# Matrix fill of a graph kernel: which engine makes the one-hots, which sums, which stores

## The reference

```python
def _L2_gnn_ref(emb, edge_weight, row, col, num_layers):
    w = edge_weight[:, None]
    X = emb
    for _ in range(num_layers):          # 3
        msgs = w * X[col]                # col = dst
        X = jax.ops.segment_sum(msgs, row, num_segments=n)   # row = src
    return X
x = _layernorm(x + _L2_gnn_ref(x, edge_weight, src, dst, 3), axis=-1)
```

## Time and profile before

| | |
|---|---|
| median of three runs | 10728.15 us (10725.5 to 10730.36) |
| the profiled execution | 10736.09 us |
| its span, first to last instruction | 10734.2 us |
| mean granted clock of TensorE | 0.844 |
| busy share of the span: PE, DVE, ACT, POOL | 72%, 67%, 15%, 49% |
| fill stage | 3294 to 4591 us of the span |

### The profile page before, as it was taken

How to read it: one execution, slowest core, us unless ns; L and a number is a source line. 1 busy time by engine, 2 the same in 40 slices (tenths; PEclk the granted TensorE clock), 3 DMA queues, 4 the chain that set the end, 5 groups by cost and what they waited for, 6 DMA issues and landing times. The chain is left out here.

```text
span 10734.2 us, 171530 instructions
## 1 busy us (share of the span) xinstructions
PE 7773.0 (72%) x33251; PEld 5843.1 (54%) x33252; DVE 7167.4 (67%) x12981; ACT 1583.2 (15%) x4852; POOL 5236.8 (49%) x6235
## 2 busy tenths in 40 slices
PE   0888869899987777756666649866664986666488
PEld 0788859788874444423444426644442664444256
DVE  2233346799955666601888779778876987888688
ACT  0222211233320000001111111211110121111011
POOL 1677720477735777700777700077771006777100
PEclk9999999899975555566999869799986988999698
DMA  5333341122231222274555641055565105555510
GB/s 23 52 61 60 61 51 40 37 46 46 46 26 65 91 91 91 91 294 177 137 137 137 129 84 37 31 133 137 137 133 89 37 26 129 137 137 136 92 40 23
DMA packets 1413038, 947.03 MB, mean 88 GB/s; under 512 B 916255, under 2 KB 1276696, under 8 KB 1412435
## 3 DMA queue, kind: packets, MB, share of 16 engines
q0 software_dynamic: 184960, 458.42, 19.9%
q1 hardware_dynamic: 1131794, 427.96, 17.0%
q10 hardware_dynamic: 96192, 59.54, 1.7%
HBM read 697.23 MB, written 248.11 MB: 88 GB/s over the span
## 5 line engine op out<-in xcount | busy, mean ns | idle before, releaser
L845 PE MATMUL ps<-rows,ohT 128*128 x7040 | 2173.4, 449 | 1348.3 <-DMA gx<-table_g,gi 670.8
L629 POOL DMA_INDIRECT gx<-table_g,gi x2640 | 2500.6, 947 | 806.0 <-issue 726.9
L845 PEld LDWEIGHTS ps<-rows,ohT 128*128 128x128 f32 x7040 | 1444.5, 248 | 1917.0 <-DMA gx<-table_g,gi 980.9
L1134 PE MATMUL ps<-work,oh 128*128 128x273 f32 (+1 forms) x7040 | 1780.1, 409 | 346.0 <-DVE oh L648 340.1
L1134 PEld LDWEIGHTS ps<-work,oh 128*128 128x128 f32 x7040 | 1342.8, 228 | 782.3 <-issue 436.1
L614 POOL COPY gi<-src_i 128x16 int32 (+1 forms) x280 | 57.4, 205 | 2476.1 <-POOLq L508 2413.8
L1630 PE MATMUL ps<-oh 128*128 128x196 f32 x2352 | 1007.9, 584 | 290.7 <-DVE oh L1597 287.1
L734 DVE TENSOR_TENSOR work<-gx,ps 128x768 f32<-128x768 f32 x660 | 629.9, 954 | 732.3 <-PE ps L847 731.8
L1099 DVE TENSOR_TENSOR work<-rows,xl 128x1024 f32<-128x1024 f32 (+1 forms) x880 | 871.6, 990 | 321.5 <-DMA xl<-xs_g 145.7
L795 ACT CAST ohT<-ps 128x512 f32<-128x512 bf16 x888 | 520.4, 586 | 3639.8 <-PE ps L828 3636.9
L1619 POOL TENSOR_SCALAR oh<-gx,lin 128x196 f32<-128x196 f32 x1176 | 902.7, 780 | 286.0 <-PE ps L1630 284.6
(11 more groups left out here) (305 smaller groups left out, 8744.7 us busy)
## 6 DMA issues: line engine op xcount, KB each, us to landing
big<-dense_d SPq DMA_DIRECT2D x96, 784.0 KB
dense_d<-big SPq DMA_DIRECT2D x588, 98.0 KB
dense_d<-big ACTq DMA_DIRECT2D x588, 98.0 KB
gx<-table_g,gi POOLq DMA_INDIRECT x2640
xs_g<-gx SPq DMA_DIRECT2D x660, 64.0 KB
xl<-xs_g SPq DMA_DIRECT2D x660, 64.0 KB, 1.8
rows<-dense_d SPq DMA_DIRECT2D x48, 784.0 KB
type_d<-work SPq DMA_DIRECT2D x220, 96.0 KB
```

What stands on the lines that cost most here:

```text
L629: pool.indirect_dma_start(m.gx[:, u, k, 0:w], None, table, bass.IndirectOffsetOnAxis(m.gi[:, odd, u * K + k:u * K + k + 1].bitcast(U32), 0 ...
L845: ins = nc.tensor.matmul(to, turned, rows, start=True, stop=not adds)
L1134: ins = nc.tensor.matmul(sums(u), m.oh[:, u, k, :], rhs(u % 2)[:, k, :], start=(k == 0), stop=(k == K - 1))
```

## The change

The fill is spread anew over the engines.

- ScalarE makes the row one-hots, without weights, in two ACTIVATEs each: `far = Square(iota + bias)` with the bias the negated key, then `spots = Relu(1 - far)`, which is 1 where the two are equal and 0 elsewhere. Every turn it first copies four keys to `lin`. So that the bias is ready, `dense_plan` writes `v_key` negated (same instruction, other signs).
- GpSimd's column one-hot takes the weight as a second operation, `is_equal` then `mult`, and copies four weights per turn beside the four numbers.
- VectorE only sums. The order one-hot, sum is gone from its queue.
- SyncE issues all four stores of a turn. It reads the four home numbers of a turn with one call at the head of the turn, and its loop is not written out for the first two turns. ScalarE issues no store.

TensorE's product waits for `spot` in place of `hot`, otherwise it stays as it was.

```diff
@@ -1518,8 +1518,8 @@
             nc.vector.tensor_copy(m.v_home[:, :], home)
             dve.wait_ge(s("picked"), 1)
             for k in range(3):
-                nc.vector.scalar_tensor_tensor(out=m.v_key[:, third(k)], in0=win_no[:, third(k)], scalar=-float(P),
-                                               in1=bank(3 + k), op0=ALU.mult, op1=ALU.add).then_inc(s("v_keys"), 1)
+                nc.vector.scalar_tensor_tensor(out=m.v_key[:, third(k)], in0=win_no[:, third(k)], scalar=float(P),
+                                               in1=bank(3 + k), op0=ALU.mult, op1=ALU.subtract).then_inc(s("v_keys"), 1)
 
         @block.scalar
         def _(act):
@@ -1570,7 +1570,10 @@
     spots = m.one_hots[:, 0:RING * P].rearrange("p (n q) -> p n q", n=RING)
     at = RING * P
     his = m.one_hots[:, at:at + RING * HIS].rearrange("p (n h) -> p n h", n=RING)
+    at += RING * HIS
+    far = m.one_hots[:, at:at + RING * P].rearrange("p (n q) -> p n q", n=RING)
     sums = m.big[:, 0:RING * HIS].rearrange("p (n h) -> p n h", n=RING)
+    numbers, weights, keys = m.lin[:, 0, 0:RING], m.lin[:, 0, RING:2 * RING], m.lin[:, 1, 0:RING]
     turns = VISITS // RING
 
     def before(u):
@@ -1582,7 +1585,7 @@
 
         @block.vector
         def _(dve):
-            def add(i, u):
+            def body(i, u):
                 v = i * RING + u
                 dve.wait_ge(s("made"), v + 1)
                 need(dve, s("summed"), v)
@@ -1590,67 +1593,67 @@
                 nc.vector.scalar_tensor_tensor(out=sums[:, u, :], in0=sums[:, before(u), :],
                                                scalar=m.v_keep[:, bass.ds(v, 1)], in1=m.ps[:, u, 0:HIS],
                                                op0=ALU.mult, op1=ALU.add).then_inc(s("summed"), 1)
-
+            nc.vector.memset(sums[:, RING - 1, :], 0.0).then_inc(s("blank"), 1)
+            dve.wait_ge(s("blank"), 1)
+            groups(dve, body, turns)
+
+        @block.scalar
+        def _(act):
             def body(i, u):
                 v = i * RING + u
-                need(dve, s("made"), v - RING + 1)
-                nc.vector.tensor_scalar(spots[:, u, :], m.iota_row[:, :], m.v_key[:, bass.ds(v, 1)],
-                                        m.v_w[:, bass.ds(v, 1)], ALU.is_equal, ALU.mult).then_inc(s("hot"), 1)
-                if u:
-                    add(i, u - 1)
-                elif not isinstance(i, int) or i:
-                    add(i - 1, RING - 1)
-            nc.vector.memset(sums[:, RING - 1, :], 0.0)
-            groups(dve, body, turns)
-            add(turns - 1, RING - 1)
+                if not u:
+                    need(act, s("far"), v)
+                    nc.scalar.copy(keys, m.v_key[:, bass.ds(v, RING)]).then_inc(s("keys"), 1)
+                    act.wait_ge(s("keys"), i + 1)
+                need(act, s("spot"), v - RING + 1)
+                nc.scalar.activation(far[:, u, :], m.iota_row[:, :], ACT.Square, bias=keys[:, u:u + 1]
+                                     ).then_inc(s("far"), 1)
+                act.wait_ge(s("far"), v + 1)
+                need(act, s("made"), v - RING + 1)
+                nc.scalar.activation(spots[:, u, :], far[:, u, :], ACT.Relu, bias=m.ones[:, 0:1], scale=-1.0
+                                     ).then_inc(s("spot"), 1)
+            groups(act, body, turns)
 
         @block.gpsimd
         def _(pool):
-            numbers = m.lin[:, 0, 0:RING]
-
             def body(i, u):
                 v = i * RING + u
                 if not u:
                     need(pool, s("high"), v)
                     nc.gpsimd.tensor_copy(numbers, m.v_hi[:, bass.ds(v, RING)]).then_inc(s("numbers"), 1)
-                    pool.wait_ge(s("numbers"), i + 1)
+                    nc.gpsimd.tensor_copy(weights, m.v_w[:, bass.ds(v, RING)]).then_inc(s("numbers"), 1)
+                    pool.wait_ge(s("numbers"), 2 * (i + 1))
                 need(pool, s("made"), v - RING + 1)
                 pool.sem_inc(s("place"), 1)
-                nc.gpsimd.tensor_scalar(his[:, u, :], m.hi_no[:, :], numbers[:, u:u + 1], None, ALU.is_equal
-                                        ).then_inc(s("high"), 1)
+                nc.gpsimd.tensor_scalar(his[:, u, :], m.hi_no[:, :], numbers[:, u:u + 1], weights[:, u:u + 1],
+                                        ALU.is_equal, ALU.mult).then_inc(s("high"), 1)
             groups(pool, body, turns)
 
         @block.tensor
         def _(pe):
             def body(i, u):
                 v = i * RING + u
-                pe.wait_ge(s("hot"), v + 1)
+                pe.wait_ge(s("spot"), v + 1)
                 pe.wait_ge(s("high"), v + 1)
                 need(pe, s("summed"), v - RING + 1)
                 nc.tensor.matmul(m.ps[:, u, 0:HIS], spots[:, u, :], his[:, u, :], start=True, stop=True
                                  ).then_inc(s("made"), 1)
             groups(pe, body, turns)
 
-        def store(eng, slots):
-            def body(i, u):
-                if u not in slots:
-                    return
-                v = i * RING + u
-                home = eng.value_load(m.v_home[0:1, bass.ds(v, 1)], min_val=0, max_val=NWIN + RING - 1)
-                eng.wait_ge(s("summed"), v + 1)
-                eng.dma_start(m.dense_d.rearrange("(w p) h -> w p h", p=P)[bass.ds(home, 1)].rearrange("a p h -> (a p) h"),
-                              sums[:, u, :]).then_inc(s(f"stored{u}"), 16)
-            groups(eng, body, turns)
-            for u in slots:
-                eng.wait_ge(s(f"stored{u}"), 16 * turns)
-
         @block.sync
         def _(sp):
-            store(sp, (0, 2))
-
-        @block.scalar
-        def _(act):
-            store(act, (1, 3))
+            view = m.dense_d.rearrange("(w p) h -> w p h", p=P)
+
+            with sp.Fori(0, turns, 1) as i:
+                _, homes = nc.values_load_multi_w_load_instructions(
+                    m.v_home[0:1, bass.ds(i * RING, RING)], engines=(mybir.EngineType.SP,), min_val=0,
+                    max_val=NWIN + RING - 1)
+                for u, home in enumerate(homes):
+                    sp.wait_ge(s("summed"), i * RING + u + 1)
+                    sp.dma_start(view[bass.ds(home, 1)].rearrange("a p h -> (a p) h"), sums[:, u, :]
+                                 ).then_inc(s(f"stored{u}"), 16)
+            for u in range(RING):
+                sp.wait_ge(s(f"stored{u}"), 16 * turns)
 
 
 def dense_layers(nc, m):
```

## The result

The changed kernel takes 10846.8 us (median of 4 runs, 10843.2 to 10850.0) against 10729.3 us of the kernel before: a ratio of 1.011 [1.0093, 1.0128]. It is 117.5 us slower; the forecast was 10668 us. The profiled execution took 10845.4 us, with a span of 10843.5.

What follows compares the result with a forecast made beforehand. VectorE's queue order, looping with PE, was taken as the bound at 4.41 us a turn; SyncE's 4.2 us over 294 turns saves 62 us, plus 2: 10736.1 to 10676, less 7.9 to the median, 10668 us; range 10575 to 10930.

Steps and rivals of the forecast that it cites:

- The bound before: VectorE's in-order queue of one-hot, sum, one-hot, sum in a loop with PE: 2.17 us per two visits, 2.21 measured.
- GpSimd: GpSimd's turn in the fill: second weight copy adds 0.19 us, second one-hot operation free, so 3.9 to 4.0 us.
- The middle bound of 0.16 us: GpSimd's second operation priced as one more pass at plain-cast rate: 0.16 us per one-hot, a turn of 4.6 us.
- Rival 3: Slower: GpSimd's second operation is paid per element, turn 4.6 us, 10786 us, tail to 11520; chance 0.15.
- SyncE: One queue for all stores and home numbers, one call per turn: 4.2 us a turn, bounds 3.3 and 5.6.
- Rival 1: Slower: SyncE's one call is really four separate reads, turn 5.5 us, 11050 us; chance 0.08.
- rival 2: Slower: SyncE's one load fetches four registers in turn, up to 0.278 us each, turn 5.0 us, 10910 us; chance 0.08.
- ScalarE: Two chained ACTIVATEs per visit plus a copy per turn on ScalarE: 3.9 us a turn, ends 3.3 and 4.5.
- Rival 4: Slower: ScalarE's chain of ACTIVATEs reaches its upper end, turn 4.5 us, 10756 us; chance 0.07.
- VectorE, PE and the landing of stores: None is the next bound: VectorE 2.8 us, PE at most 3.5 us, landing 3.0 us, under a 4.2 us turn.
- The sum: The slowest of GpSimd, ScalarE and SyncE sets the fill's turn: 4.2 us, gaining 62 us less 2 us.
- the side that had 0.38: The outcome slower than the kernel before, rivals 1 to 4 together: chance 0.38.

## Why the prediction was wrong

**The bound before** was read rightly. The sum one place later gave 10535 us by changing nothing but the order of the earlier trace rows, and landed on GpSimd's 3.70 us a turn.

**GpSimd** is the step that failed. "3.9 to 4.0 us if the second operation is free" was taken; it measured 4.79. The second copy cost less than said, 0.12 us in place of 0.19: the two overlap. The whole miss is the second operation, 0.17 us, and its operand, 0.08 us, times four. My ground for "free", that the pass is slow already and so does both in any case, was an argument and not a row, and the measured one-hots refute it. The middle bound of 0.16 us from the cast of the earlier trace rows came out near the price of the operation with an immediate (0.17); whether for its reason was not tried. What it left out was the operand, though ScalarE's row with a bias from SBUF stood beside it with 0.09 us for the same thing. With 0.25 us per one-hot and 0.12 for the copy, the turn of 3.70 us that the sum began with gives 4.8. Rival 3 named the mechanism and its threshold, 0.90 us per one-hot, rightly; it put 4.6 us on it (10786 us) and had a chance of 0.15, too low for the one term whose row was missing.

**SyncE** was right. After, its work without waits is 4.80 - 177.4/294 = 4.19 us a turn; with GpSimd out of the way it set 4.22. The range check, taken at the 0.152 us of its longest step, cost 0.24 with the small steps around it; the bound of 3.3 us without checks held, at 3.26. Rival 1 would have cost 5.34 (5.5 said), and it was not the case. For rival 2, the load of four registers takes 0.17 us more than that of one, so 0.06 us for each further register and not 0.278. The Trainium skill, "Runtime: NRT & Kernel Launch", section "Instruction fetch mechanics", has some 200 ns per register also in bulk; for a read from SBUF of four registers side by side the measured 436 ns decides against it. The 10845 us that rival 2 has by that figure lie beside the measured 10847 by luck: they put the loss on SyncE, which still waited 177 us.

**ScalarE** was put too high, without harm: 3.9 us said, 3.3 measured. Early in the stage of the run without the range check, where ScalarE's code is that of the changed kernel, it went through a turn without waiting for PE:

```profile
3302.64 0.19 ACT L1606 COPY lin<-big 128x4 f32 x1
3302.95 0.40 ACT L1609 ACTIVATE oh<-iota_row,lin 128x128 f32<-128x128 f32 x1
3303.38 0.40 ACT L1613 ACTIVATE oh<-oh,ones 128x128 f32<-128x128 f32 x1
3303.69 0.39 ACT L1609 ACTIVATE oh<-iota_row,lin 128x128 f32<-128x128 f32 x1
...
3305.95 0.19 ACT L1606 COPY lin<-big 128x4 f32 x1
```

An ACTIVATE takes 0.39 to 0.40 us, as said. The gap ahead of the second of a pair, which I took as 0.10, is 0.03 us (3303.35 to 3303.38), the lower bound from the earlier trace rows. The next pair starts 0.31 us after the second, while it still runs. So a pair takes 0.73 us and the copy adds 0.39: 4 x 0.73 + 0.39 = 3.31 us, the lower end of the prediction. With the waits for PE this gives the turns that were measured: 3.31 + 132.2/294 = 3.76 us in that run, 3.31 + 441.1/294 = 4.81 us in the changed kernel. There ScalarE had 1.5 us a turn to spare. Rival 4 did not happen.

**VectorE, PE and the landing of stores** stayed off the path in the changed kernel, as said. But the prediction held that landing stays covered at a turn of 4.2 us, and at 4.22 us, with SyncE full, VectorE's sums waited 606 us for it. It was the follower: the stores were late because their queue was, and without the range check these waits were gone.

**The sum** had one bad term. With GpSimd's 4.79 in it, 10728 + 294 x (4.79 - 4.41) + 2 is 10842 us, and 10847 was measured. That lies within the range of 10575 to 10930 us, on the side that had 0.38.

## What to carry to other kernels

Before work is spread over engines, ask whether the engines are full or only wait for each other in a loop: here none was full, one step of a queue's order was worth 1.9%, and the spreading 0.45% once its costly part was mended. A fused second operation is free only where a row of that engine says so: on GpSimd it made each one-hot a third longer, and the engine it was moved to was the next bound. When three engines come out within 10% of each other, the term without a row of its own can decide the sign.

## What the runs showed of the hardware

- GpSimd's tensor_scalar of 128x196 f32 took 773 ns with one operation, 941 with a second one by an immediate, 1022 with a second one by a scalar from SBUF. That is 3.9, 4.8 and 5.2 ns per element, against 0.83 for the cast. The Trainium skill, "GPSIMD Engine Reference", section "Engine selection", calls operations with one input roughly line-rate; for this one the runs show about a fifth of the cast's rate.
- VectorE made the same column one-hot in 322 ns.
- An ACTIVATE of 128x128 took 401 ns with a bias from SBUF and 493 with bias and scale from SBUF, 0.09 us for the second operand as for the first.
- One register load of four numbers took 436 ns, of one 264; the range check took 0.24 us of the queue per number.
- An ACTIVATE that waits for the one ahead of it on ScalarE started 0.03 us after its end; one that does not wait for it started 0.31 us after its start, 0.09 us before its end.
- A wait that the profile puts down to another engine can be the engine's own: GpSimd's 0.28 us ahead of a turn's one-hots stands under its copies in the changed kernel and under PE in the run without the range check.
- The granted clock, mean of 3350 to 4150 us, was 0.50 before, in the changed kernel and with the second operation alone, 0.53 with the immediate, 0.56 with four reads, 0.60 to 0.66 without the second operation, with the weight on ScalarE, without the range check and with the sum one place later, and 1.00 with the column one-hot on VectorE. It does not follow the turn's length alone (0.50 at 4.41 us, 0.56 at 5.34), nor PE's busy share (78% at 0.50 and at 1.00). It explains no part of the loss, since it was 0.50 on both sides.
